# Masking all four heads of the first attention in one VectorE operation

## The reference

```
x = x + linear_attention(layernorm(x))     # 16 heads of 8, causal, elu+1 features
x = x + moe(layernorm(x))                  # 16 experts (top 4) and 2 shared ones
x = x + softmax_attention(layernorm(x))    # 16 heads of 8
x = x + moe(layernorm(x))
```

```
S = S + pk_t[..., :, None] * v_t[..., None, :]
z = z + pk_t
num = einsum('bhd,bhde->bhe', pq_t, S)
den = sum(pq_t * z) + EPS
out_t = num / den
```

## Time and profile before

| | us |
|---|---|
| median of 3 executions | 665.49 |
| lowest, highest | 659.54, 668.21 |
| the profiled execution's own time | 655.46 |
| its span | 653.7 |
| first product to last mask of the first attention (start times) | 36.0 to 128.9 |

### The profile page before, as it was taken

The page is one execution under the profiler, slowest core; times in us unless marked ns, Lnnn a source line. Parts: engine busy times, 40 slices in busy tenths (PEclk is TensorE's granted clock), DMA queues, the critical chain, the costliest instruction groups (busy, mean ns, idle before and its releaser), DMA issues. The chain is left out here.

```text
span 653.7 us, 12112 instructions
## 1 busy us (share of the span) xinstructions
PE 574.5 (88%) x4045; PEld 426.0 (65%) x4045; DVE 453.9 (69%) x1089; ACT 345.3 (53%) x580; POOL 378.1 (58%) x356
## 2 busy tenths in 40 slices
PE   1768988888999999995897897989887999999996
PEld 1656666667888888883454454555556788888884
DVE  5646759858688896672645575669858779697574
ACT  1344565445555655552444564758573655555553
POOL 4367887445666667667444455655314665666664
PEclk9999999979999999999558898999798999999999
DMA  7002200042344344320000000000022334433341
GB/s 182 1 2 74 75 1 3 10 76 95 104 109 128 90 124 114 106 88 1 1 1 1 2 1 2 2 1 2 2 56 68 106 99 132 135 104 123 105 145 34
DMA packets 33864, 40.88 MB, mean 63 GB/s; under 512 B 4994, under 2 KB 17299, under 8 KB 33811
## 3 DMA queue, kind: packets, MB, share of 16 engines
q1 hardware_dynamic: 30704, 39.73, 21.5%
q10 hardware_dynamic: 3106, 0.48, 0.4%
HBM read 38.88 MB, written 1.31 MB: 61 GB/s over the span
## 5 line engine op out<-in xcount | busy, mean ns | idle before, releaser
L523 POOL TENSOR_TENSOR KS<-PT,QS 128x512 fp32r<-128x512 f32 x144 | 185.9, 1291 | 125.1 <-ACT QS L684 115.2
L679 ACT ACTIVATE bank<-bank 128x512 f32<-128x512 f32 x128 | 74.5, 582 | 109.7 <-PE bank L702 109.1
L1374 DVE TENSOR_TENSOR PT<-CS,bank 128x512 f32<-128x512 f32 x128 | 87.6, 684 | 48.7 <-PE bank L702 48.3
L1277 DVE TENSOR_REDUCE MEXP<-bank 128x4 f32<-128x1024 f32 x64 | 78.2, 1224 | 56.0 <-PE bank L805 56.0
L700 PE MATMUL bank<-XH,WH 128*128 128x512 f32 (+1 forms) x288 | 115.8, 402 | 0.8 <-DVE PT L1257 0.8
L702 PE MATMUL bank<-XH,WL 128*128 128x512 f32 (+1 forms) x288 | 113.6, 394 | 0.0
L701 PE MATMUL bank<-XL,WH 128*128 128x512 f32 (+1 forms) x288 | 113.4, 394 | 0.0
L613 ACT ACTIVATE PT<-bank 128x1024 f32<-128x1024 f32 x64 | 65.5, 1023 | 68.5 <-PE bank L837 68.3
L1379 DVE TENSOR_TENSOR PT<-PT,bank 128x512 f32<-128x512 f32 x128 | 88.1, 688 | 10.6 <-ACT bank L679 2.4
L684 ACT ACTIVATE QS<-PT 128x512 fp32r<-128x512 f32 x144 | 90.1, 626 | 4.2 <-DVE PT L1379 3.8
L475 POOL TENSOR_TENSOR HP<-PHI,COL 128x512 fp32r<-128x512 f32 x32 | 33.3, 1040 | 71.6 <-ACT PHI L601 71.6
(11 more groups left out here) (173 smaller groups left out, 967.5 us busy)
## 6 DMA issues: line engine op xcount, KB each, us to landing
CS<-combine_rows SPq DMA_DIRECT2D x128, 256.0 KB, 3.2
out_dram<-X SPq DMA_DIRECT2D x4, 256.0 KB, 3.9
stage<-in_L_ffn_gate_w_dram SPq DMA_DIRECT2D x5, 192.0 KB, 2.6
stage<-in_L_ffn_up_w_dram SPq DMA_DIRECT2D x5, 192.0 KB, 2.9
stage<-in_L_ffn_down_w_dram SPq DMA_DIRECT2D x5, 192.0 KB, 4.4
X<-in_L_attn_a_x_dram SPq DMA_DIRECT2D x1, 768.0 KB, 6.3
X<-in_L_attn_a_x_dram SPq DMA_DIRECT2D x1, 256.0 KB, 3.3
combine_rows<-CB SPq DMA_DIRECT2D x8, 32.0 KB, 2.5
```

The lines of the kernel that those rows point to most:

```text
L523: pool.tensor_tensor(GL[:, (u - 1) % 3, :], GG[:, (u - 1) % 3, :], GH[:, (u - 1) % 3, :].bitcast(f32), ALU.subtract).then_inc(F.gl, 1)
L679: act.activation(TH[:, u, :] if u < SHARED else G[u % 3][:, :], G[u % 3][:, :], ACT.Silu).then_inc(F.th, 1)
L1277: dve.tensor_reduce(top, S4[:, 2 * x:2 * x + 2, :].rearrange("p h (t k) -> p h t k", t=2), AX.X, ALU.max).then_inc(A.mx[x], 1)
L1374: dve.tensor_tensor(ab, CS[:, e % CBUFS, :], U[u % 3][:, :], ALU.mult).then_inc(F.b, 1)
```

## The change

VectorE's mask takes all four heads: one operation over four banks, 384 columns each, waiting for the fourth head's `s1`. ScalarE's copy of head 3, GpSimd's product and their semaphores `h3` and `pm` go, and so do the waits of TensorE on them. MASK, the buffers and the rest stay.

```diff
@@ gpsimd, slot @@
-                def masked_scores(i):
-
-                    part = PT[:, i % 2, 3, 0:3 * P].rearrange("p (a b) -> p a b", a=3)[:, 0:3:2, :]
-                    pool.wait_ge(A.h3, i + 1)
-                    pool.tensor_tensor(part, part, MASK[:, 0:3:2, :], ALU.mult).then_inc(A.pm, 1)
...
-                    if 0 <= n - 3 < ITEMS:
-                        masked_scores(n - 3)
@@ scalar, slot @@
-                def last_head(i):
-
-                    act.wait_ge(A.s1, 4 * i + 4)
...
-                    act.activation(PT[:, i % 2, 3, 0:3 * P], S[3][:, 0:3 * P], ACT.Copy).then_inc(A.h3, 1)
...
-                    if 0 <= n - 3 < ITEMS:
-                        last_head(n - 3)
@@ tensor, products @@
                         if i and h == 0:
                             pe.wait_ge(A.mk, i)
-                        if i and h == 3:
-                            pe.wait_ge(A.h3, i)
@@ tensor, values_product @@
                         pe.wait_ge(A.mk, i + 1)
-                        pe.wait_ge(A.pm, i + 1)
@@ vector, masked_scores @@
-                    dve.wait_ge(A.s1, 4 * i + 3)
+                    dve.wait_ge(A.s1, 4 * i + 4)
...
-                    dve.tensor_tensor(PT[:, i % 2, 0:3, 0:3 * P], S4[:, 0:3, 0:3 * P],
+                    dve.tensor_tensor(PT[:, i % 2, :, 0:3 * P], S4[:, :, 0:3 * P],
                                       MASK[:, :, :].rearrange("p a b -> p (a b)").unsqueeze(1)
-                                      .broadcast_to([P, 3, 3 * P]), ALU.mult).then_inc(A.mk, 1)
+                                      .broadcast_to([P, 4, 3 * P]), ALU.mult).then_inc(A.mk, 1)
```

More of the change, by code:

```diff
@@ L53, in __init__ @@
             self.kx = sem(prefix + "kx")
-            self.h3 = sem(prefix + "h3")
-            self.pm = sem(prefix + "pm")
             self.mk = sem(prefix + "mk")
@@ L584, in features @@
                     act.activation(bank[:, :], bank[:, :], ACT.Relu).then_inc(A.rl, 1)
-                def last_head(i):
-                    act.wait_ge(A.s1, 4 * i + 4)
-                    if i >= 2:
-                        act.wait_ge(A.pv, i - 1)
-                    elif i == 0:
-                        act.wait_ge(s_qkl, 1)
-                    act.activation(PT[:, i % 2, 3, 0:3 * P], S[3][:, 0:3 * P], ACT.Copy).then_inc(A.h3, 1)
                 def rows(p):
@@ L992, in unit @@
                             pe.wait_ge(A.mk, ITEMS)
-                            pe.wait_ge(A.h3, ITEMS)
                             pe.wait_ge(s_wl, PIECES)
```

## The result

The median went from 661.0 us (20 executions, 654.95 to 669.91) to 669.91 us (20 executions, 664.95 to 683.14): a ratio of 1.0153, 95% interval 1.0119 to 1.0188. The ratio, here and in the experiments, is taken over the ordinary executions of each kernel, without the few that are over 1.5% above its fastest; by it the kernel is 10.1 us slower (7.9 to 12.4), by the plain medians 8.9. That is slower, by less than the 2% named in the prediction; 672 us was forecast. The profiled execution took 670.29 us, 14.8 more than the one of before. Of these 14.8 only part belongs to the change, as the table shows (spans between starts, in us; the "first attention" runs from the first mask's start to the first expert matmul's).

A forecast was written before the change was run, and what follows sets the result against it. The prediction took TensorE and VectorE waiting on each other over the score banks as the first attention's bound. Mask costs of +10.1 us less 2.4 us relief gave +7.7 us: 673.2 against the median, 672 us taken, range 664 to 682.

The forecast's parts named there:

- The ring: First attention: TensorE's products and VectorE's mask wait for each other over one set of score banks, 2.55 us a turn.
- The wider mask: VectorE's mask in the first attention goes from 1152 to 1536 columns, costing 0.40 us more each.
- The later start: VectorE's mask waits for the fourth head's products, not the third's: 0 to 0.06 us a turn, 0.02 taken.
- 24 steps: Of 32 first-attention steps, mask to mask or last mask to expert matmul, 24 grow by 0.42 us: +10.1 us.
- 6 full: Steps where VectorE has no idle time before the next mask, so a longer mask pushes everything: 0.42 us each.
- the three covered ones: Steps from masks at 73.65, 91.09 and 123.06, where TensorE's own work hides the longer mask: no cost.
- the step with SC: Step around 101 to 102 us where VectorE's small operations leave no idle time: 0.42 us longer.
- The relief: TensorE's waits on GpSimd's queue that go: 1.6 us before values products, 0.8 before products needing keys CS; -2.4 us.
- The fresh draw of neighbours: VectorE's small operations meeting different GpSimd operations on shared ports: taken as nothing, at most 0.96 us either way.
- From the profile to the median: Carrying +7.7 us from the profiled 655.46 us to the 665.49 median: 673.2 by the sum, 672 us taken.
- Rival 1: TensorE's clock falls in the first attention as longer turns leave it less busy: 679 to 682 us; chance 0.12.
- Rivals 2 and 3: Relief of TensorE's waits offsets the mask, 665 us, chance 0.12; freed ports speed VectorE, below 652 us, chance 0.02.

## Why the prediction was right, and where it was not

**The ring as the bound.** Right. Four runs changed one side of it each, and the turn followed: 2.60 with a later start, 2.60 with three banks and the later start, 2.55 with four heads but an early release, 2.09 to 2.29 with a mask of 0.96 us.

**The wider mask, 0.40.** Right: 1.754 against 1.355 us. Three banks instead of four give back 0.40 of the turn and 7.5 us of the stage.

**The later start, 0.02 taken between 0 and 0.06.** The term was too small: 0.06 a turn, shown with the mask's width unchanged. The reason given (that the 0.06 of the earlier trace rows would be ScalarE's own start) was wrong; VectorE needs all of it. In the 17 turns of the ring, where 0.42 was forecast and 0.455 measured, it makes the 0.6 us between +7.1 and +7.7.

**24 steps.** Right in number and kind: 17 of the ring, 6 full, 1 at the end; the three covered ones moved by 0.01 or less. One of the full ones, the step with SC, became 0.15 shorter instead: SC took 0.18 us, since XV no longer stood beside it, and then TensorE's 3.65 us of own work set the step.

**The relief, -2.4.** Right: -2.6, with the step of the earlier trace rows at -1.19 (forecast -1.2), and no wait of the values product on GpSimd left.

**The fresh draw of neighbours, taken as nothing, at most 0.96 either way.** This is the term that was mis-sized most, though what it came to in all was small. Two operations that had been undisturbed at 0.17 and 0.23 us became 0.91 and 1.01, ME went from 0.93 to 1.17, and others went the other way: SC from 1.15 to 0.18, W from 0.65 to 0.23. The bound was set by one operation, and the queue that was loosened had several: the text counted GpSimd's 32 masks as possible neighbours, and not that they held the first key back and kept the others apart. In the five full steps the new neighbours cost 1.3 us net, over the bound of 0.96; the step with SC came out 0.57 better than forecast. The two together are +0.7, inside the bound again, but that they cancel in part is luck. The rule in the Trainium skill (SBUF — State Buffer, Who interferes with whom), that VectorE and GpSimd share ports which one of them holds for a whole instruction, is borne out by the run: 0.91 beside the key, 0.17 without it. But the conclusion drawn from it, that fewer GpSimd operations can only help VectorE, was false: with 32 fewer the small operations in the full steps were stretched by 2.7 us and not by 1.4.

**From the profile to the median.** The forecast's base, 672 - 7.7 = 664.3, was 3.3 above the 661.0 that 20 executions gave; the sum was 1.2 under the 8.9 between the medians, and 2.4 under the 10.1 of the ratio, just below its interval (7.9 to 12.4). The total came out only 2.1 from the forecast because base and sum err against each other, and that is luck. In the stage itself the sum was 0.9 under the 8.6 measured; what the rest of the 10.1 is stays open.

**Rival 1, the clock.** Not what decided, but its price was nearly right. At the low clock a turn takes 3.73, +0.73 where 0.6 was said. In the kernel after only the first turn had it, so the sign that the prediction named for this rival (a granted clock below 1.00 between 36 and 131 us) did show, from 37.3 to 44.2 us, and cost 0.7 us. What speaks against the rival's mechanism: the clock was already low before the longer turns began (from 37.3 us after, 36.1 to 56.6 with keys on ScalarE), and it was low there with the short turns of the kernel before too, in the run with a later start (36.3 to 43.1). In the kernel before, too, the first products of the stage (at 35.98) took 1.26 us; the clock rose only after them, and the 1.00 of the earlier trace rows holds from 37.7 us on. From the sixth step on the turns of 3.00 ran at 2.4 GHz in the kernel after and with the keys on ScalarE. The Trainium skill (TensorE: Matmul & The Clock Gate, Part 1) lets an idle window alone throttle; the waits of 1.26 us inside the ring did not, which agrees. But the clock also fell in three runs where VectorE is full and TensorE's waits are longer: from 122.9 us with three heads and one, both with the keys on GpSimd and on ScalarE, and from 127.6 to 131.0 with all of GpSimd paced, after waits of 1.51, 0.67 and 1.17 us:

```profile
127.53 1.26 PE L750 MATMUL bank<-PQ,CS 32*128 32x256 f32 x8 [1.17 <-DVE PT L1234]
```

In none of the three was TensorE idle for over 1.93 us at a time in the 10 us before the fall. The kernel after had waits up to 1.70 us in its full steps and kept 2.4 GHz. So a fall of the clock inside this stage does occur, outside the plain turns, and what decides it is open. Whether long turns keep a low clock low for longer is open: of the four profiled runs with the long turn two had one low turn of 3.73 at the start and two had four, and of the ten with a short turn none had more than two there. **Rivals 2 and 3** fell: the turns did not stay at 2.55, and nothing sped up by more than the 2.6 named.

## What to carry to other kernels

In a ring of two engines over one buffer, what counts is the time between the last write and the release of the first part, not how much work an engine has. Here four heads cost nothing more in the ring once the first three were released early (a turn of 2.55 us, as with three heads). Moving work onto such an engine also needs the stretches where it has no idle time, for there every operation counts. And work taken off another queue lets that queue run together: ask which operations it kept apart, and beside whom they land now.

## What the runs showed of the hardware

- Some small VectorE operations that read SBUF alone and take 0.17 to 0.23 us take up to 1.31 us beside a GpSimd operation of 512 columns (0.91, 1.01, 1.17 and 1.31 above), and end when that one does. They are TENSOR_TENSOR and SCALAR_TENSOR_TENSOR (T, W), the COPY to ME, and TENSOR_SCALAR (SC). MATCH_REPLACE8, which reads SBUF alone too, is not stretched: it took 0.15 us each from 118.38 to 118.94 in the kernel after, while keys ran from 117.20 to 120.24. Nor is the mask, which reads PSUM as one of its inputs: 1740 to 1758 ns in all 32, though keys overlap several.
- GpSimd needs 1.04 us for a key, ScalarE 0.71 on average; its activations of 512 columns from PSUM take 0.59 to 0.60 us, so a key took longer there than had been expected. Why it is slower there is open.
- The recorded clock can be incomplete: in the run with the keys held back, TensorE's eight matmuls took 1.26 us as at 1.2 GHz (0.74 at 2.4), while the granted clock of that stretch reads 1.00 (the profile's first clock record of this run is at 55.3 us). TensorE's timeline of that run:

```profile
43.43 1.26 PE L748 MATMUL bank<-PQ,CS 32*128 32x256 f32 x8 [0.61 <-DVE PT L1232]
```

and its stretch:

```profile
44.00:48.00 4.00, 3.39 (x40) 2.24 (x36) 1.76 (x1) 1.38 (x2) 2.63 (x2) 1.00 0.00 0
```

The length of a known group of matmuls is the surer sign.
